# An adaptive-normalisation attention and feed-forward layer: shift weights on ScalarE's queue, first products in turn, weight parts and batch 1's order changed

## The chip, the cores and the metric

One core of a Trainium2 chip. The metric is the device time of one execution, in microseconds (us). The time before is 363.78 us, the median of three runs (363.32 to 365.0).

## What is computed

Four batches of 512 tokens with 512 features, all in float32. `c` (4 x 512) gives six rows per batch: shift and scale of the attention part, its gate, and the same for the feed-forward part.

```python
mod = (_silu(c) @ wmod).reshape(4, 6, 1, -1)
sa, ca, ga, sb, cb, gb = (mod[:, i] for i in range(6))
ga, gb = ...                               # sign kept, magnitude at least 0.25
h = _layernorm(x) * (1 + ca) + sa
x = x + ga * attn(h)
h = _layernorm(x) * (1 + cb) + sb
x = x + gb * ffn(h)
# attn: Xn = layernorm(h)*gamma+beta; Q, K, V = Xn @ W_in + b_in; K, V turned by rotary
#   A = sum over tokens of cos_sim(K) * cos_sim(V); A = 0.5*A + 0.5
#   (A * Q) @ W_out + b_out + h
# ffn: relu(x @ W_up.T) @ W_down.T + (sum of the two top routing weights) * (x @ W_expert)
```

## The kernel before

TensorE multiplies in a float32 form of reduced precision, so each product is three: every operand is split into a high part (a rounded copy, written by ScalarE or GpSimd) and a low part (the rest, written by VectorE or GpSimd), and hi x hi, hi x lo and lo x hi are added. Weights are split in four parts of 128 rows (k = 0 to 3), tokens stand in four tiles of 128 (t = 0 to 3).

Every engine has its own hand-written order, and semaphores alone tie them. SyncE (SP) issues all transfers in the order of its program. The stages are: a start, attention of batches 0 to 3, feed-forward of batches 0 to 3. On TensorE attention(b) is: K/V tile 0 of batch b, the four output rows of batch b-1, K/V tiles 1 to 3, four Q chunks with the eight transposes of batch b+1 between them, and the sums that give A. Tile 3 uses the pair of banks of tile 1, and waits for VectorE's last product step of tile 1 (`krot`, L873); the transposes of chunks 2 and 3 (L1284) wait for the same step of tile 3.

The start. For batch 0 the scale and shift rows are computed on every partition by TensorE from the column `sc0` (silu of c): `mod_first` (L1233 to L1237) does four products for the scale row (bank 2) and then four for the shift row (bank 3), each as two matmuls in full float32. Each product waits for its own 256 KB part of the weights (`ca_w`, `sa_w`). ScalarE adds one to the scale row (L711), VectorE takes the statistics of token rows (`x0_stats`, L1051 to L1056), forms (x - mean) * scale (`scale_row0`, L1061) and then h = that * rstd + shift (`h_row0`, L1074); VectorE's order is statistics of rows 0, scale_row0(0), statistics of rows 1, h_row0(0). Then come second statistics, GpSimd's reciprocal root (L411), z on ScalarE (L626), TensorE's transposes (L1270), gamma and beta (L585), the high copy (L588) and the low split (L842) that the first K/V product needs.

The weights of K and V come in eight parts. High copies are ScalarE's (`split_hi_kv`, L577), low parts GpSimd's (`low_kv`, L414), except part 2 of K, which is VectorE's (`split_lo_kv`, L1079).

Batch b+1's x is normalised in two steps during attention(b). The first: statistics, root on GpSimd (`rstd_x`), shift factors on VectorE (`x_shift`), z on ScalarE (`normalise_x`, L617); GpSimd multiplies by ca (`scale_rows`, L470), VectorE adds sa (`h_row`, L815), and the second normalisation follows. Batch 3's first step is done early, within attention(1): ScalarE sums rows and squares with accumulating passes (`x_sums`, `x_squares`, L596 and L604), VectorE forms mean and variance (L793, L797), and ScalarE writes its z at the end of its attention(1), ahead of batch 1's q evacuation (L648). Meanwhile GpSimd also finishes half of the output rows of batch b-1 (`x2_out`, L453 and L455).

## Time and profile before

| | |
|---|---|
| median of the timed runs | 363.78 us |
| the profiled execution's own time | 365.14 us |
| its span | 363.4 us |
| TensorE busy | 353.1 us |
| VectorE, ScalarE, GpSimd busy | 247.9, 159.1, 126.6 us |
| granted TensorE clock | full speed throughout |

The span runs from the first to the last recorded instruction; a little of the execution lies around it. TensorE is the engine to watch: where it doesn't wait, nothing that other engines do moves the end. In the timeline each line has a start and a duration in us, and in brackets how long the engine idled ahead of it and what released it; "issue" there is a release that the profile doesn't name. A shared port or a lock shows as the same instruction with a longer duration.

### The profile page before, as it was taken

What the parts mean: (1) busy time and instruction counts of PE and PEld (TensorE: products, weight loads), DVE (VectorE), ACT (ScalarE), POOL (GpSimd) and SP (SyncE); (2) the same over time, 40 slices, a digit from 0 to 9 for tenths busy, and PEclk for the clock granted to TensorE, in tenths of its full rate; (3) what the DMA queues carried; (4) which work ended last, traced back from release to release, by engine and by line L of the source; (5) the groups of instructions that cost most, each with busy time, mean ns of one, the idle gap of its engine ahead of it and who ended that gap; (6) DMA issues with size and microseconds to landing.
All of it is one profiled execution on the core that took longest, in us unless ns stands there. A gap on an engine that the chain in (4) does not pass through costs nothing.

```text
span 363.4 us, 4952 instructions
## 1 busy us (share of the span) xinstructions
PE 353.1 (97%) x1794; PEld 288.5 (79%) x1794; DVE 247.9 (68%) x508; ACT 159.1 (44%) x301; POOL 126.6 (35%) x131
## 2 busy tenths in 40 slices
PE   8799999999999999999999999999999999999996
PEld 5257587788777788888888898988988898889885
DVE  2689999979977778786977469338623852382474
ACT  1296838647169501476018753444234423441110
POOL 0395879777726166243531324800100010000000
PEclk9999999999999999999999999999999999999999
DMA  6998482370120000000000003101100110011003
GB/s 182 388 406 317 194 318 89 137 213 0 25 63 2 0 2 29 1 1 2 0 31 0 0 2 115 32 0 58 60 0 2 58 59 2 0 60 58 2 1 115
DMA packets 10985, 27.45 MB, mean 76 GB/s; under 512 B 1216, under 2 KB 1600, under 8 KB 9808
## 3 DMA queue, kind: packets, MB, share of 16 engines
q1 hardware_dynamic: 10960, 27.13, 21.1%
q8 instruction: 14, 0.23, 0.3%
q14 instruction: 11, 0.09, 0.1%
HBM read 22.90 MB, written 4.23 MB: 75 GB/s over the span
## 4 chain that ended last, share of the span: by engine, by line
PE 60%; DVE 12%; ACT 8%; issue 7%; DMA 5%; POOL 5%; SPq 2%; POOLq 0%; DVEq 0%; ACTq 0%
PE ps L1225 19%; PE ps L1227 19%; PE ps L1226 19%; PE ps L1284 2%; DMA gate_bc<-mod_rows 2%; DMA xs<-in_X 2%; POOL w_lo L414 2%; DVE hb L815 1%; DVE hst L825 1%; ACT z L626 1%; POOL hrs L411 1%; ACT ps L638 1%; DMA mod_rows<-xs 1%; ACT ps L585 1%; ACT z L617 1%
## 5 line engine op out<-in xcount | busy, mean ns | idle before, releaser
L1225 PE MATMUL ps<-wv_hi,t_hi 128*128 128x260 f32 (+1 forms) x192 | 61.7, 322 | 0.9 <-POOL wv_lo L414 0.5
L1227 PE MATMUL ps<-wv_hi,t_lo 128*128 128x260 f32 (+1 forms) x192 | 61.4, 320 | 0.0
L1226 PE MATMUL ps<-wv_lo,t_hi 128*128 128x260 f32 (+1 forms) x192 | 61.4, 320 | 0.0
L1225 PE MATMUL ps<-w_hi,g_hi 128*128 128x512 f32 (+1 forms) x132 | 51.2, 388 | 0.0
L1225 PE MATMUL ps<-t_hi,w_hi 128*128 128x512 f32 x128 | 50.6, 396 | 0.1
L1227 PE MATMUL ps<-w_hi,g_lo 128*128 128x512 f32 (+1 forms) x132 | 50.6, 383 | 0.0
L1226 PE MATMUL ps<-w_lo,g_hi 128*128 128x512 f32 (+1 forms) x132 | 50.6, 383 | 0.0
L1227 PE MATMUL ps<-t_hi,w_lo 128*128 128x512 f32 x128 | 50.0, 390 | 0.0
L1226 PE MATMUL ps<-t_lo,w_hi 128*128 128x512 f32 x128 | 49.9, 390 | 0.0
L1225 PEld LDWEIGHTS ps<-wv_hi,t_hi 128*128 128x128 f32 x192 | 36.1, 188 | 5.1 <-POOL wv_lo L414 1.4
L411 POOL TENSOR_TENSOR hrs<-hve,expo 128x4 f32<-128x4 f32 (+2 forms) x12 | 11.1, 923 | 81.9 <-DVE hve L832 62.8
L1227 PEld LDWEIGHTS ps<-wv_hi,t_lo 128*128 128x128 f32 x192 | 36.1, 188 | 2.9
L1226 PEld LDWEIGHTS ps<-wv_lo,t_hi 128*128 128x128 f32 x192 | 36.1, 188 | 2.8
L1225 PEld LDWEIGHTS ps<-w_hi,g_hi 128*128 128x128 f32 x132 | 24.8, 188 | 5.1 <-DVE g_lo L907 0.5
L1227 PEld LDWEIGHTS ps<-w_hi,g_lo 128*128 128x128 f32 x132 | 24.8, 188 | 4.9
L1226 PEld LDWEIGHTS ps<-w_lo,g_hi 128*128 128x128 f32 x132 | 24.8, 188 | 4.7
L1227 PEld LDWEIGHTS ps<-t_hi,w_lo 128*128 128x128 f32 x128 | 24.0, 188 | 5.1
L1225 PEld LDWEIGHTS ps<-t_hi,w_hi 128*128 128x128 f32 x128 | 24.1, 188 | 5.0 <-issue 0.4
L1142 DVE SCALAR_TENSOR_TENSOR g_lo<-ps,g_hi 128x512 fp32r<-128x512 f32 x16 | 11.1, 692 | 24.7 <-ACT g_hi L655 24.6
L1226 PEld LDWEIGHTS ps<-t_lo,w_hi 128*128 128x128 f32 x128 | 24.1, 188 | 4.7
L571 ACT ACTIVATE sqj<-ps 128x512 bf16<-128x512 f32 x16 | 9.5, 591 | 41.5 <-DVE ps L854 36.5
L1225 PE MATMUL ps<-w_hi,t_hi 128*128 128x512 f32 x64 | 26.1, 408 | 1.2 <-DVE prod L873 0.9
(153 smaller groups left out, 703.8 us busy)
## 6 DMA issues: line engine op xcount, KB each, us to landing
stage<-in_w SPq DMA_DIRECT2D x5, 1024.0 KB, 4.8
out<-xs SPq DMA_DIRECT2D x15, 256.0 KB, 2.0
xs<-in_X SPq DMA_DIRECT2D x3, 1024.0 KB, 9.5
xs<-in_wmod SPq DMA_DIRECT2D x8, 256.0 KB, 5.9
stage<-in_w SPq DMA_DIRECT2D x8, 256.0 KB, 8.1
xs<-in_wmod SPq DMA_DIRECT2D x2, 1024.0 KB, 7.7
gate_bc<-mod_rows SPq DMA_DIRECT2D x8, 256.0 KB, 3.9
gate_bc<-in_wmod SPq DMA_DIRECT2D x1, 1024.0 KB, 13.3
```

Of the source, the lines that this page charges most:

```text
L411: nc.gpsimd.tensor_tensor(hrs[:, t0:t0 + n], hve[:, t0:t0 + n], expo[:, 0:n], ALU.pow).then_inc(hrs_s, n)
L414: nc.gpsimd.tensor_tensor(w_lo_of(W_ORDER[i], k), w_raw[i][:, k * D:(k + 1) * D], w_hi_of(W_ORDER[i], k).bitcast(f32), ALU.subtract).then_ ...
L571: nc.scalar.activation(sqj[:], src, ACT.Square, accum_out=nsq[:, t % 2, i:i + 1]).then_inc(nsq_s, 1)
L585: nc.scalar.activation(part, part, ACT.Identity, bias=col[:, COL_BETA + c:COL_BETA + c + 1], scale=col[:, COL_GAMMA + c:COL_GAMMA + c + 1] ...
L617: nc.scalar.activation(z[:, t, :], xs[:, tok(g, t)], ACT.Identity, bias=xnm[:, t:t + 1], scale=xrs[:, t:t + 1]).then_inc(xn_s, 1)
L626: nc.scalar.activation(z[:, t, :], src, ACT.Identity, bias=hnm[:, t:t + 1], scale=hrs[:, t:t + 1]).then_inc(z_s, 1)
L638: nc.scalar.activation(whole, whole, ACT.Identity, bias=bias, scale=scale).then_inc(t_full, 1)
L1142: v.scalar_tensor_tensor(g_lo[:, c, :], ps[:, U_BANKS[c % 2], :], 0.0, g_hi[:, c, :].bitcast(f32), ALU.max, ALU.subtract).then_inc(u_los, 1)
L1225: mm(dst, l_hi, r_hi, start=start, stop=False)
L1226: mm(dst, l_hi, r_lo, start=False, stop=False)
L1227: return mm(dst, l_lo, r_hi, start=False, stop=stop)
L1284: last = nc.tensor.transpose(ps[:, t_bank(g, c), t * P:(t + 1) * P], z[:, t, c * P:(c + 1) * P], idn[:])
```

## The change

SP issues two scale parts, then token rows 0, two scale parts and token rows 1, and no shift parts. ScalarE issues the four shift parts on its own queue ahead of everything else it does. TensorE's first products go scale 0, shift 0, scale 1, shift 1, scale 2, scale 3, then shift 2, shift 3; the scale row is signalled after six products.

GpSimd does K's low part 1 ahead of the root for token rows 2 and 3. V's low part 3 goes from GpSimd to VectorE, between h_row0(3) and the split of transposed rows 1. ScalarE copies V's high part 1 ahead of z of rows 1. One wait in `split_lo_kv` stands twice.

Batch 3's first normalisation moves from attention(1) to attention(2), and is done as batch 2's: statistics on VectorE between q splits, root on GpSimd behind batch 2's bias rows, z on ScalarE behind the first sums. ScalarE's eight accumulating passes and VectorE's mean and variance go. In batches 1 and 2, h row 0 of the next batch goes from behind the sum of tile 0 to behind the product step of tile 1.

```diff
             sp.dma_start(col[:], cols).then_inc(col_in, 16)
...
+            load_scale(0)
+            load_scale(1)
             load_x0(0)
-            for k in range(NC):
-                sp.dma_start(x_slot(3)[:, k * D:(k + 1) * D], wmod[0][:, k * D:(k + 1) * D]).then_inc(sa_w[k], 16)
+            load_scale(2)
+            load_scale(3)
             load_x0(1)
...
                     weight(b, 1)
-                    if b + 2 < B:
-                        rstd_x(b + 2)
                     rstd_h(b + 1, 0, NT)
...
                     for t in range(NT):
                         base(b + 1, t)
+                    if b == 1:
+                        rstd_x(3)
...
             shift_h0(1)
+            low_kv(0, 1)
             rstd_x0(2)
-            low_kv(0, 1)
             low_kv(1, 1)
             low_kv(1, 2)
             low_kv(0, 3)
-            low_kv(1, 3)
             shift_h0(2)
...
                 norm_sums(b, 0)
-                if b == 1:
-                    normalise_x(2)
-                    x_sums()
-                    x_squares()
+                if b < B - 1:
+                    normalise_x(b + 1)
                 norm_sums(b, 1)
...
                     t_evac(b + 1, c)
-                if b + 2 < B:
-                    normalise_x(b + 2)
+            for k in range(NC):
+                nc.scalar.dma_start(x_slot(3)[:, k * D:(k + 1) * D], wmod[0][:, k * D:(k + 1) * D]).then_inc(sa_w[k], 16)
             act.wait_ge(col_in, 16)
...
             split_hi_kv(0, 1)
+            split_hi_kv(1, 1)
             normalise(0, 1, 1)
-            split_hi_kv(1, 1)
...
                 for c in range(NC):
                     q_split(b - 1, c)
-                    if b == 1:
-                        x_row_stats(2, c)
-                if b == 1:
-                    x_aggr(2)
+                    if b < B - 1:
+                        x_row_stats(b + 1, c)
+                if b < B - 1:
+                    x_aggr(b + 1)
                 kv_rows(b, 0)
                 kv_products(b, 0)
-                if b == 1:
-                    x_shift(2)
+                if b < B - 1:
+                    x_shift(b + 1)
...
                 finish_rows(b - 1)
-                if b == 1:
-                    x_mean()
                 kv_sum(b, 0)
-                if b < B - 1:
-                    h_row(b + 1, 0)
-                else:
+                if b == B - 1:
...
                 kv_rows(b, 1)
-                if b == 1:
-                    x_var()
                 kv_products(b, 1)
                 if b < B - 1:
+                    h_row(b + 1, 0)
                     h_row(b + 1, 1)
...
                 kv_products(b, 2)
-                if b + 2 < B:
-                    x_shift(b + 2)
                 kv_sum(b, 2)
...
                 dve.wait_ge(whi_v if i else whi_k, k + 1)
+                dve.wait_ge(wlo_v if i else wlo_k, k)
                 dve.wait_ge(wlo_v if i else wlo_k, k)
...
             h_row0(3)
+            split_lo_kv(1, 3)
             t0_split(1)
...
+            def first_rows():
+                for k in range(2):
+                    first_scale(k)
+                    first_shift(k)
+                for k in range(2, NC):
+                    last = first_scale(k)
+                last.then_inc(bc_ps, 1)
+                for k in range(2, NC):
+                    last = first_shift(k)
                 last.then_inc(bc_ps, 1)
...
-            mod_first(2, x_slot(2), ca_w)
-            mod_first(3, x_slot(3), sa_w)
+            first_rows()
```

## Rows read from the trace of the kernel before

**Rows 1.** busy time (us and share of the span) and instructions of each engine
```profile
PE 353.1 (97%) x1794; PEld 288.5 (79%) x1794; DVE 247.9 (68%) x508; ACT 159.1 (44%) x301; POOL 126.6 (35%) x131
```

**Rows 2.** waits of TensorE's weight loads, 90 to 125 us: total, times, longest
```profile
PEld ps L1225 <- issue: 1.3, 1, 1.3
PEld ps L1284 <- issue: 1.0, 1, 1.0
PEld ps L1284 <- ACT z L626: 0.9, 1, 0.9
PEld ps L1225 <- DVE g_lo L907: 0.5, 1, 0.5
```

**Rows 3.** the same view, 20 to 66 us
```profile
PEld ps L1225 <- POOL wv_lo L414: 1.4, 2, 0.7
```

**Rows 4.** timeline of the first 15 us: start, duration, engine, line, operation
```profile
2.63 0.22 ACT L708 ACTIVATE sc_t<-col 128x16 f32<-128x16 f32 x1 [0.62 <-DMA col<-in_cols]
...
3.54 2.14 SPq L298 DMA_DIRECT2D xs<-in_wmod  x4
...
5.43 3.66 PE L1236 MATMUL ps<-xs,prod 128*128 128x512 f32 x8
...
9.19 0.75 ACT L711 ACTIVATE ps<-ps,half 128x512 f32<-128x512 f32 x1 [6.34 <-PE ps L1236]
...
10.41 3.70 PE L1236 MATMUL ps<-xs,prod 128*128 128x512 f32 x8 [1.33 <-DMA xs<-in_wmod]
...
13.17 0.69 DVE L1051 BATCH_NORM_STATS2 xst<-xs 128x6 f32<-128x512 f32 x1 [2.45 <-DMA xs<-in_X]
...
14.22 0.75 DVE L1074 SCALAR_TENSOR_TENSOR hb<-hb,xrs,ps 128x512 f32<-128x512 f32 x1
```

**Rows 5.** stretches: busy time by engine, clock, DMA share, GB/s
```profile
0.00:7.00 7.00, 5.90 (x14) 4.06 (x15) 1.48 (x10) 1.50 (x2) 0.52 (x5) 1.00 0.63 181
7.00:9.00 2.00, 2.00 (x5) 0.57 (x3) 0.43 (x1) 0.00 (x0) 0.00 (x0) 1.00 0.79 180
9.00:12.00 3.00, 1.67 (x5) 0.86 (x5) 1.35 (x4) 0.75 (x1) 0.56 (x1) 1.00 1.03 386
```

**Rows 6.** timeline, 20 to 29 us
```profile
20.56 0.71 POOL L381 TENSOR_TENSOR xrs<-xve,expo 128x2 f32<-128x2 f32 x1
...
21.36 1.30 POOL L414 TENSOR_TENSOR w_lo<-stage,w_hi 128x512 fp32r<-128x512 f32 x1
...
24.11 0.68 DVE L1079 TENSOR_TENSOR w_lo<-stage,w_hi 128x512 fp32r<-128x512 f32 x1
...
24.30 1.66 POOL L414 TENSOR_TENSOR wv_lo<-stage,wv_hi 128x512 fp32r<-128x512 f32 x1 [0.38 <-ACT wv_hi L577]
...
28.50 0.19 PEld L1225 LDWEIGHTS ps<-wv_hi,t_hi 128*128 128x128 f32 x1 [0.71 <-POOL wv_lo L414]
```

**Rows 7.** timelines of VectorE and GpSimd, 87 to 98 us
```profile
87.60 1.50 POOL L455 TENSOR_TENSOR xs<-xs,hb 128x512 f32<-128x512 f32 x1
87.86 1.79 DVE L815 TENSOR_TENSOR hb<-hb,sa_bc 128x512 f32<-128x512 f32 x1
...
93.61 0.42 DVE L873 TENSOR_TENSOR prod<-ps,rot_sb 128x256 f32<-128x256 f32 x1
...
96.37 1.27 DVE L815 TENSOR_TENSOR hb<-hb,sa_bc 128x512 f32<-128x512 f32 x2
```

**Rows 8.** timeline of ScalarE, 104 to 117 us
```profile
104.37 1.51 ACT L626 ACTIVATE z<-hb,hnm,hrs 128x512 f32<-128x512 f32 x2
...
113.93 2.92 ACT L617 ACTIVATE z<-xs,xnm,xrs 128x512 f32<-128x512 f32 x4
```

**Rows 9.** timeline of VectorE, 137 to 158 us
```profile
137.43 0.70 DVE L854 TENSOR_TENSOR ps<-ps,bkv_bc 128x512 f32<-128x512 f32 x1 [2.57 <-PE ps L1227]
...
156.85 0.42 DVE L873 TENSOR_TENSOR prod<-ps,rot_sb 128x256 f32<-128x256 f32 x1
```

**Rows 10.** the chain that ended last: start, duration, piece
```profile
157.61 0.88 PE ps L1284 x8
```

More of the change, by code:

```diff
@@ L102, in build @@
         nmu = xmn
-        xss = sb("xss", [P, NT])
         xst = sb("xst", [P, NT, 6])
@@ L288, in _, with load_scale @@
             sp.dma_start(col[:], cols).then_inc(col_in, 16)
-            for k in range(NC):
+            def load_scale(k):
                 sp.dma_start(x_slot(2)[:, k * D:(k + 1) * D], wmod[1][:, k * D:(k + 1) * D]).then_inc(ca_w[k], 16)
@@ L294, in load_x0 @@
                              x_batch[0][:, rows0, :]).then_inc(x0_in[i], 16)
+            load_scale(0)
+            load_scale(1)
             load_x0(0)
-            for k in range(NC):
-                sp.dma_start(x_slot(3)[:, k * D:(k + 1) * D], wmod[0][:, k * D:(k + 1) * D]).then_inc(sa_w[k], 16)
+            load_scale(2)
+            load_scale(3)
             load_x0(1)
@@ L589, in t0_evac @@
                                      ACT.Copy).then_inc(t_his, 1)
-            def x_sums():
-                act.wait_ge(x_in, (B - 1) * 16)
-                for t in range(NT):
-                    wait(act, xsum_s, t)
-                    nc.scalar.activation(xjunk[:], xs[:, tok(B - 1, t)], ACT.Identity,
-                                         accum_out=xsum[:, t:t + 1]).then_inc(xsum_s, 1)
-            def x_squares():
-                act.wait_ge(xmn_s, 1)
-                for t in range(NT):
-                    act.wait_ge(xsum_s, NT + t)
-                    nc.scalar.activation(xjunk[:], xs[:, tok(B - 1, t)], ACT.Square, bias=xmn[:, t:t + 1],
-                                         accum_out=xss[:, t:t + 1]).then_inc(xsum_s, 1)
             def normalise_x1(t):
@@ L1231, in idle_products, with first_scale, first_shift @@
                     mm(ps[:, IDLE_BANK, 0:2 * P], acc[:, 0:P], acc[:, 0:2 * P], start=True, stop=True)
-            def mod_first(bank, src, sems):
-                for k in range(NC):
-                    pe.wait_ge(sems[k], 16)
-                    last = mm(ps[:, bank, :], sc0[:, k, :], src[:, k * D:(k + 1) * D], start=(k == 0), stop=(k == NC - 1))
+            def first_scale(k):
+                pe.wait_ge(ca_w[k], 16)
+                return mm(ps[:, 2, :], sc0[:, k, :], x_slot(2)[:, k * D:(k + 1) * D], start=(k == 0), stop=(k == NC - 1))
+            def first_shift(k):
+                pe.wait_ge(sa_w[k], 16)
+                return mm(ps[:, 3, :], sc0[:, k, :], x_slot(3)[:, k * D:(k + 1) * D], start=(k == 0), stop=(k == NC - 1))
+            def first_rows():
[7 more added lines that the diff above has]
+                    last = first_shift(k)
                 last.then_inc(bc_ps, 1)
```

15 lines of the change are left out of this document (1 added, 14 removed).

## The prediction

> **What bounds the kernel now.** I read the table of busy time first: TensorE is busy in 97% of the span [rows 1]. So time can only come from three places: before its first real product, from its waits, or after its last one. The tail is untouched by this change. The waits of its weight loads in the stretch of batch 1 are few: 1.3 us, 1.0, 0.9 and 0.5, 3.7 us in all [rows 2]. In the start, the loads wait 1.4 us more for the low parts of V's weights [rows 3]. Then I read the timeline of the first 15 us: the first token rows become h at 14.22, and everything up to the first K/V product hangs on that as one serial chain over VectorE, GpSimd, ScalarE and TensorE (statistics, root, z, transposes, evacuation, split). So the change has some 6 us to work on, in three places, and in each I ask what is late next.
>
> **Part 1, the first rows (start of h at 14.22).** Before, four scale products are over when ScalarE adds one at 9.19; the four shift products start at 10.41, take 3.70 us (0.9 each) and end at 14.1. VectorE gets its second token rows only at 13.17, takes three short steps (0.69 and two more, about 1.05 to 14.22) and starts h [rows 4]. Two things are thus late together: the shift row at 14.1, and the statistics of token rows 1, which stand ahead of h in VectorE's order.
>
> The change removes the four shift issues from SP's queue (2.14 us for four, 0.54 each [rows 4]) so what is behind them is issued up to 2.1 us sooner, and puts them on ScalarE ahead of its exponential. That began at 2.63 after 0.62 us of idling [rows 4], so it moves by up to 2.14 - 0.62 = 1.5 us; TensorE's first product was at 5.4 and becomes some 0.2 to 0.4 later, 5.7. What it adds on the path is order: TensorE now does scale, shift, scale, shift, scale, scale before the scale row is ready. That is six products instead of four, so at best 5.7 + 6 x 0.9 = 11.1 instead of 9.1. Behind it stand ScalarE's 0.75, VectorE's product of the same kind as that at 14.22 (0.75), and then the 1.05 of statistics that used to be done while VectorE waited for data: 11.1 + 0.1 + 0.75 + 0.75 + 1.05 = 13.8. The best case is -0.4.
>
> Whether TensorE can run at that pace is a matter of bytes. Bandwidth was 181 GB/s over the first 7 us, 180 in the next two and 386 after [rows 5]: 1.27 MB by 7.0, 1.63 by 9.0, 2.79 by 12.0. The transfers up to token rows 1 are 2.65 MB, so their bytes were in by 11.6 and the wait for them ended at 13.17: 1.5 us between byte and wait. Shared evenly by two queues, the last scale part comes after all shift parts and token rows 0, at 2.36 MB instead of 1.05. By the old curve that is 10.9 + 1.5 = 12.4, last scale product over at 13.3, and h at 13.3 + 2.7 = 16.0: +1.8. If the slow stretch of 7 to 9 us vanishes because both queues are in flight early, it lands near 10.8 to 11.2. The trace has no second queue, so both ends stay. I take a landing of 10.8, a last scale product ending at 11.8, h at 14.5: **+0.3** (range -0.4 to +1.8). The Trainium skill (DMA: Bandwidth & Descriptors, "Issuing engines are not separate DMA queues") says that transfers of all issuing engines run on the same 16 engines and interleave, so that a second issuer saves only the time of issuing. No second issuer is in this trace to agree or not; by that rule the late end, with nothing but issue time gained, is the more natural, and it is a rival below.
>
> **Part 2, the order of weight parts.** GpSimd did the reciprocal root for token rows 2 and 3 at 20.56 (0.71 us), in time it had anyway, since K's part 1 could start only at 21.36. Now it waits for that part, works 1.30 on it and does the root at 22.6 to 23.3. VectorE's h of token rows 2 becomes 1.1 us later, and with it VectorE's part 2 of K (24.11). That then meets GpSimd's V part 2, which already took 1.66 instead of 1.30 beside it [rows 6]; I let it wait to 25.9 and end at 26.5, 1.7 late. K's part 3 on GpSimd waits for it and ends at 26.5 + 1.3 = 27.8. Against that, V's part 3 (1.30 on GpSimd, 0.68 on VectorE) leaves GpSimd, where it let TensorE wait 0.71 before the product at 28.50 [rows 6], and lies on VectorE behind h of token rows 3 (27.95) and ahead of the split of t: ready at 28.65, the split at 29.3. The second tile starts at 29.4 where it started three products after 28.50, at 29.1: **+0.3**. Without the collision each step is 0.6 earlier and it is -0.3. Taking V's part 1 before the second normalisation costs nothing: TensorE transposes those rows only after part 0's six products. The repeated wait is one that is already met.
>
> **Part 3, batch 1.** Eight ScalarE passes over batch 3, the mean and the variance go from here; their successor is four statistics on VectorE between batch 1's q splits. What TensorE waited 1.3 us for [rows 2] is VectorE's product step ending at 93.61 + 0.42 = 94.03 [rows 7]. Ahead of that step VectorE loses the mean (0.9), the variance and one h row of 1.79 (the row of 87.86), so it ends near 91.3, 2.7 sooner, and this wait of 1.3 is gone whole. But what is next? That h row is not gone, it comes right behind the step, where GpSimd has four or five products in a row. A VectorE instruction whose two inputs are both in SBUF took 1.79 beside GpSimd's at 87.60, and 1.27 for two, 0.64 each, with none beside it [rows 7]. Going through both engines' orders by turns: h row 0 ends at 92.6, h row 1 at 94.4, GpSimd's last scaling moves by 1.0 to 95.7, h rows 2 and 3 end at 96.9 instead of 97.64. So of 2.7 us only some 0.8 survive. z of batch 2, ending at 105.88 [rows 8], released the transposes (the 0.9 wait); it moves by 0.8, and TensorE, now 1.3 ahead, waits again. The 1.0 wait, for tile 3's product step, gives 0.1 more since the shift for batch 3 went from there. Part 3 is **-0.9** (range -0.65 to -2.05; the far end is no collision at all). The Trainium skill (SBUF — State Buffer, "Who interferes with whom") has it that a VectorE instruction with two SBUF inputs and a GpSimd instruction that reads SBUF shut each other out whole. The trace agrees (1.79 against 0.64), and it speaks against this move of the h row.
>
> **Part 4, batch 3's normalisation out of ScalarE's way.** Its 2.92 us stood at 113.93, right ahead of batch 1's q work [rows 8]. Gone from there, q can begin once its scale is ready, about 0.7 sooner; the splits keep ScalarE's pace with the statistics between, as the trace of batch 0 has them. TensorE's wait of 0.5 for the last split goes: **-0.4** (range 0 to -0.4). The normalisation is now in batch 2 behind the first sums, where ScalarE idles; the new 0.45 of aggregation lies on VectorE before tile 0 of batch 2, which TensorE doesn't wait for.
>
> **Part 5, the price in batch 2.** The same h row was in VectorE's idle time there: it idled 2.57 before the K rows of 137.43 [rows 9]. Now it comes behind the product step and moves all that follows by 0.64. GpSimd's chain gets 0.3 easier or harder. Tile 3's product step ended at 156.85 + 0.42 = 157.27 and TensorE's transposes went at 157.61 [rows 9, 10]: cover 0.2 to 0.3. It comes 0.3 to 0.9 late: **+0.5** (range +0.1 to +0.9). TensorE's other work in batches 2 and 3 and the feed-forward part hangs on nothing that changed.
>
> **Sum.** +0.3 + 0.3 - 0.9 - 0.4 + 0.5 = -0.2. The profiled execution took 365.14 us, of which 363.4 is its span; the median of the timed runs is 363.78, 1.4 below it. The change acts within the span: 363.4 - 0.2 = 363.2, and 363.78 - 0.2 = **363.6** for the median.
>
> **Rivals.** (a) The engines don't collide as I let them. Part 3 is then -2.05 (limited by z of batch 2), part 2 -0.3, part 5 +0.1, part 1 0, part 4 -0.4: -2.65, 361.1. For it: only some of VectorE's instructions show the long form. Against: every h row beside GpSimd does. (b) The scale row comes late. Its place is TensorE's order: the last two scale products now stand behind two shift products, and share bandwidth with all four shift parts. Its price is +1.8 in part 1, sum +1.3, 365.1; it makes part 1 a loss from the point where the sixth product ends after 11.5, and the whole a loss from about 11.9. This is the skill's rule of one set of engines taken at its word. (c) The second queue doesn't do what it is for: its shift parts land no sooner than before, when the first let TensorE begin at 10.41 and the second was used 0.9 later [rows 4]. Then shift 1, scale 2 and scale 3 follow from 11.3, the scale row is done at 14.0, h starts 2.7 later at 16.7, +2.5, sum +2.0, 365.8.
>
> **Chances.** My sum 0.52, (a) 0.28, (b) 0.13, (c) 0.07. The range takes in (a) and (b) and stops at (c): 361.0 to 365.6. A measurement here can tell about 0.5% (1.8 us) from no change. Faster by more needs most of (a): 0.28. Slower by more needs (c), or (b) with the bad end of part 2 or 5: 0.13. Within: 0.59.
>
> **What would show it.** Part 1: the ends of the sixth and eighth first products (11.8, 13.7) and the start of h (14.5). Part 2: K's part 2 on VectorE late by over 1 us, the second tile near 29.4 plus the shift of part 1. Part 3: no wait at 94, but one of about 0.9 before the transposes near 105. Part 4: no wait in the first output rows of batch 1. Part 5: a new wait of about 0.5 before the transposes near 157. I am wrong at once if VectorE's h rows in batch 1 run at 0.64 beside GpSimd, or if TensorE's first six products end by 11.1.

## The result, and the profile after

The changed kernel takes 367.56 us (median of 5 runs, 366.93 to 367.82) where the kernel before took 363.78 (362.38 to 365.0): 1.009 times as long, with an interval of 1.0072 to 1.0108. It is 3.8 us slower by the medians and 3.3 by the ratio, which is taken over more runs of the kernel before, and lies above the predicted range. Its profiled execution took 367.82 us with a span of 365.9.

Its busy times, in the form of [rows 1]:

```profile
PE 355.1 (97%) x1794; PEld 289.7 (79%) x1794; DVE 249.8 (68%) x516; ACT 153.1 (42%) x285; POOL 124.4 (34%) x130
```

TensorE is recorded busy 2.0 us longer for the same 1794 instructions, and again 97% of the span: what is lost must be looked for in its waits and its pace, not in work that was added. The timeline of the first 17 us of after, as in [rows 4]:

```profile
0.73 1.85 ACTq L687 DMA_DIRECT2D xs<-in_wmod  x4
...
4.15 0.22 ACT L689 ACTIVATE sc_t<-col 128x16 f32<-128x16 f32 x1 [0.25 <-DMA col<-in_cols]
...
5.79 1.75 PE L1198 MATMUL ps<-xs,prod 128*128 128x512 f32 x2
...
7.38 1.02 PE L1202 MATMUL ps<-xs,prod 128*128 128x512 f32 x2
...
9.02 0.30 PEld L1198 LDWEIGHTS ps<-xs,prod 128*128 128x128 f32 x2 [1.45 <-DMA xs<-in_wmod]
...
11.38 0.30 PEld L1198 LDWEIGHTS ps<-xs,prod 128*128 128x128 f32 x2 [1.20 <-DMA xs<-in_wmod]
...
12.04 0.49 PEld L1198 LDWEIGHTS ps<-xs,prod 128*128 128x128 f32 x2 [0.37 <-DMA xs<-in_wmod]
...
13.20 1.88 PE L1202 MATMUL ps<-xs,prod 128*128 128x512 f32 x4
...
14.25 0.75 DVE L1022 SCALAR_TENSOR_TENSOR hb<-xs,xmv,ps 128x512 f32<-128x512 f32 x1 [2.61 <-ACT ps L692]
...
14.91 0.69 DVE L1012 BATCH_NORM_STATS2 xst<-xs 128x6 f32<-128x512 f32 x1
...
15.97 0.75 DVE L1035 SCALAR_TENSOR_TENSOR hb<-hb,xrs,ps 128x512 f32<-128x512 f32 x1
```

The reader sees the second queue being issued first (ACTq, 0.73 to 2.58), the exponential moved from 2.63 to 4.15, the products in pairs, and waits of the weight loads for scale parts: 1.45 us before 9.02 (part 1), 1.20 before 11.38 (part 2) and 0.37 before 12.04 (part 3). VectorE's scaling of the token rows starts at 14.25 where it was 9.97, the statistics of token rows 1 come behind it, and h starts at 15.97 instead of 14.22.

The weight parts in after, as in [rows 6] (GpSimd's root, VectorE's h of token rows 2, K's part 2, and K's part 3):

```profile
24.34 0.70 POOL L381 TENSOR_TENSOR xrs<-xve,expo 128x2 f32<-128x2 f32 x1
...
25.07 0.75 DVE L1035 SCALAR_TENSOR_TENSOR hb<-hb,xrs,ps 128x512 f32<-128x512 f32 x1 [1.19 <-POOL xrs L381]
...
26.93 1.19 DVE L1041 TENSOR_TENSOR w_lo<-stage,w_hi 128x512 fp32r<-128x512 f32 x1
...
28.26 1.30 POOL L414 TENSOR_TENSOR w_lo<-stage,w_hi 128x512 fp32r<-128x512 f32 x1 [0.69 <-DVE w_lo L1041]
```

The root and the h row that waits 1.19 for it, the 1.19 of K's part 2 beside GpSimd, and GpSimd's wait of 0.69 for it are as the prediction let them run. The waits of the weight loads from 90 to 125 us, as in [rows 2]:

```profile
PEld ps L1260 <- issue: 1.0, 1, 1.0
PEld ps L1260 <- ACT z L609: 0.7, 1, 0.7
```

The 1.3 and the 0.5 are gone, and 1.7 us stay. In batch 1 and at the end of batch 2 (VectorE's K rows, product step and h rows of batch 1; TensorE's transposes of batch 2):

```profile
91.28 0.70 DVE L822 TENSOR_TENSOR ps<-ps,bkv_bc 128x512 f32<-128x512 f32 x1 [2.67 <-PE ps L1190]
...
95.20 0.42 DVE L841 TENSOR_TENSOR prod<-ps,rot_sb 128x256 f32<-128x256 f32 x1
...
95.55 1.92 DVE L783 TENSOR_TENSOR hb<-hb,sa_bc 128x512 f32<-128x512 f32 x2
...
159.75 0.86 PEld L1260 LDWEIGHTS ps<-idn,z 128*128 128x128 f32 x8 [0.69 <-issue]
```

Two h rows beside GpSimd took 1.92 us, where two alone take 1.27 [rows 7]: the collision is there. So is the new wait near the end of batch 2, 0.69 us. And VectorE now idles 2.67 us before the K rows at 91.28, since TensorE has not made them yet.

Where the 3.8 us are: the start of single steps in the timelines (us from the span's start; the last row is an end). "h" is VectorE's first h row; all rows of transposes are TensorE's weight loads for them. "Transposes 1a, 1b" are the two groups in which TensorE transposes z of batch 1 in the middle and at the end of batch 0's attention, and so on. before (2) is a second profiled execution of the kernel before (363.72 us in all), taken with the experiments.

| step | before | before (2) | after | after less before (2) |
|---|---|---|---|---|
| h of token rows 0 | 14.22 | 14.32 | 15.97 | +1.65 |
| first K/V product | 21.55 | 21.64 | 24.53 | +2.89 |
| transposes of z, third 128 tokens | 30.48 | 30.53 | 32.28 | +1.75 |
| transposes 1a | 56.36 | 56.42 | 58.57 | +2.15 |
| transposes 1b | 60.66 | 60.72 | 64.12 | +3.40 |
| transposes 2a | 105.93 | 104.48 | 108.14 | +3.66 |
| transposes 3a | 153.61 | 152.18 | 155.48 | +3.30 |
| transposes 3b | 157.39 | 155.93 | 159.75 | +3.82 |
| end of the last product | 360.25 | 358.84 | 362.59 | +3.75 |

Three things are read from it. The loss lies in the start (+1.65) and between transposes 1a and 1b (+1.25), and +0.5 in between. The changes of batch 1 and later gave nothing (+3.40 to +3.75). And the first K/V product is 2.9 us late for a moment, of which 1.75 are left at the third tile. The stretches of after, in the form of [rows 5], and the weight loads around them:

```profile
15.00:20.00 5.00, 3.04 (x16) 0.90 (x16) 4.69 (x11) 1.82 (x3) 2.52 (x4) 1.00 1.05 388
20.00:22.00 2.00, 2.00 (x9) 0.55 (x8) 1.93 (x8) 1.68 (x6) 1.78 (x2) 0.69 1.05 402
22.00:25.00 3.00, 3.00 (x10) 2.43 (x11) 1.57 (x4) 3.00 (x6) 2.08 (x3) 0.64 1.00 410
```

```profile
19.71 0.42 PEld L1246 LDWEIGHTS ps<-idn,z 128*128 128x128 f32 x4 [2.84 <-issue]
...
21.71 2.79 PEld L1194 LDWEIGHTS ps<-acc 128*128 128x128 f32 x8 [1.28 <-issue]
...
24.53 0.19 PEld L1188 LDWEIGHTS ps<-w_hi,t_hi 128*128 128x128 f32 x1
```

Behind a gap of 2.84 us of the weight loads, ahead of 19.71, the granted clock falls to 0.69 and 0.64, a mean of time at the 1.2 GHz level (0.50) and time at 2.4 GHz, where before had 1.00 (2.4 GHz) throughout. The idle products of the load at 21.71 (products whose results nobody uses) take 2.79 us at it. What that costs is an experiment below.

### The profile page after: what moved, and what is told of

The parts are those of the page before. It is cut to its first block, busy times and chain, and to the rows that moved or that the text cites. A ratio compares the mean times of both kernels' runs of the same rounds, so it can differ in the third digit from the quotient of the medians.

```text
span 365.9 us, 4943 instructions
## 1 busy us (share of the span) xinstructions
PE 355.1 (97%) x1794; PEld 289.7 (79%) x1794; DVE 249.8 (68%) x516; ACT 153.1 (42%) x285; POOL 124.4 (34%) x130
## 4 chain that ended last, share of the span: by engine, by line
PE 59%; DVE 19%; issue 10%; ACT 5%; DMA 2%; POOL 2%; SPq 0%; POOLq 0%; DVEq 0%; ACTq 0%
PE ps L1188 19%; PE ps L1190 18%; PE ps L1189 18%; PE ps L1260 2%; DMA xs<-in_wmod 2%; DVE hb L783 2%; ACT z L609 2%; DVE prod L835 2%; DVE ps L839 1%; POOL hrs L411 1%; DVE hst L793 1%; DVE hst L787 1%; ACT sqj L570 1%; DVE acc L853 1%; ACT z L600 1%
```

## The experiments

The kernels of a group ran on one chip with runs of the kernel before beside them; its median was 363.6 to 364.5 us from group to group, so each kernel is compared with the one of its group.

**The three parts, one at a time.** start_only has the second queue, SyncE's new order and the new order of products; parts_only the new order of weight parts; batch_only all of batch 1 and later.

> Before, with only the first part: shift weights from ScalarE's queue and the eight first products in turn. Theory A (the late scale row is most of the loss): h of the first token rows starts near 16.0 instead of 14.2, TensorE is at half clock for its idle products, and the time is 2.0 to 2.6 us above before. Theory B (the weight parts are most of it, by loading VectorE in the start): the late start is mostly absorbed by the waits on weight parts, at most +1.0. Theory C (a collision of VectorE and GpSimd near 60 us adds 1.1 us, and comes only with all parts together): +1.5 to +1.9.

> Before, with only the second part: order of the weight parts. Theory A: +0.3 to +0.9, since the root of token rows 2 and 3 comes 2 us later and VectorE's part 2 of K collides with GpSimd. Theory B: +1.5 or more. Theory C: 0 to +0.3.

> Before, with only the third part: batch 3's first normalisation in attention(2) and h row 0 behind tile 1's product step in batches 1 and 2. All theories: the wait of 1.3 us near 94 goes, the one of 0.5 near 122 goes, a new one of 0.4 to 0.7 comes near 157: 0.9 to 1.3 us below before. If the start and this part depend on each other (the gate rows' round trip), it is between 0 and 0.6 below.

| kernel | median | before | ratio (interval) | difference |
|---|---|---|---|---|
| start_only | 366.29 | 364.51 | 1.0053 (1.0033 to 1.0072) | +1.9 |
| parts_only | 365.80 | 364.51 | 1.0045 (1.0029 to 1.0061) | +1.6 |
| batch_only | 364.59 | 364.51 | 1.0001 (0.9981 to 1.0020) | 0.0 |

The differences by the ratios add up to 3.5, where the whole change has 3.3 by its ratio. That they fit so well is partly chance: start_only and parts_only both contain the loss between transposes 1a and 1b, which after has only once (below). The start costs more than its likely value, the weight parts five times theirs, and batch 1 gains nothing of what all theories expected. Each needs its cause.

**The same kernels once more, for a second trace.** before_again is the kernel before, batch_again is batch_only, both unchanged.

> Before unchanged, for a second trace of it. Theory C (near 58 us VectorE's sum of tile 2 and GpSimd's low part 1 of the output weights ask for the shared port within 0.05 us of each other, so executions of before differ): this trace may show the sum at 1.0 or at 2.1 us, and the wait of 1.3 us near 94 may be missing; its end then lies 0.6 to 1.4 us before that of the first trace. If before is steady, both traces agree within 0.3 us at every stage.

> The third part alone, unchanged, for a second trace. Its profiled time lay 0.7 us under its median. If the third part really is worth 1.2 us, this trace repeats the first within 0.3 us; if it gains only against a slow execution of before, this one differs from its first trace by 0.5 us or more, in the stage before 65 us.

before_again took 363.72 us in its profiled execution, batch_again 365.14. The waits of the weight loads in before_again, 90 to 125 us:

```profile
PEld ps L1285 <- issue: 0.9, 1, 0.9
PEld ps L1285 <- ACT z L627: 0.5, 1, 0.5
PEld ps L1226 <- DVE g_lo L908: 0.5, 1, 0.5
```

The wait of 1.3 us on which part 3 rested [rows 2] isn't there. The profiled execution of before was a long one of its kind (365.14 us against a median of 363.78), and this is where it lost its time: in it VectorE had waited 1.46 us for the gate rows, which come back from memory, as this row of its timeline shows:

```profile
79.51 1.29 DVE L916 TENSOR_TENSOR hb<-ps,hb 128x512 f32<-128x512 f32 x2 [1.46 <-DMA gate_bc<-mod_rows]
```

In before_again that wait is absent, and transposes 2a start 43.76 us after 1b instead of 45.27. In all other traces of this study that distance is 43.3 to 44.0, but for late_old, below. (The sum at 57.7 us, where the expectation looked for the difference, is short in both traces of before.) Between batch_only and batch_again the difference is elsewhere, at the sum of tile 2 of batch 0 (VectorE L885 of before) against GpSimd's second low part of the out weight. before_again:

```profile
57.73 1.02 DVE L886 SCALAR_TENSOR_TENSOR acc<-prod,wgt,acc 128x768 f32<-128x768 f32 x1
57.77 2.12 POOL L407 TENSOR_TENSOR w_lo<-stage,w_hi 128x512 fp32r<-128x512 f32 x1
```

batch_again:

```profile
57.34 2.15 DVE L849 SCALAR_TENSOR_TENSOR acc<-prod,wgt,acc 128x768 f32<-128x768 f32 x1
57.39 1.29 POOL L403 TENSOR_TENSOR w_lo<-stage,w_hi 128x512 fp32r<-128x512 f32 x1
```

Both engines start within 0.05 us of each other. In the one VectorE takes 1.02 us and GpSimd's instruction is the long one (2.12 for 1.29), in the other VectorE takes 2.15. Transposes 1b follow 4.30 us after 1a in before_again and 5.56 in batch_again, and the end comes 1.2 us later than in batch_only (360.25 against 359.02). The same kernel does both, so this is decided from execution to execution. The starts don't tell which way it goes: VectorE is 0.04 to 0.05 us ahead in every trace of either form.

**Which engine goes first.** after has the long form:

```profile
59.88 2.14 DVE L853 SCALAR_TENSOR_TENSOR acc<-prod,wgt,acc 128x768 f32<-128x768 f32 x1
59.92 1.28 POOL L406 TENSOR_TENSOR w_lo<-stage,w_hi 128x512 fp32r<-128x512 f32 x1
```

after_win is after with a wait that lets VectorE's sum go first; before_win is the same in before.

```
                 pool.wait_ge(whi_out, k + 1)
+                if k == 1:
+                    pool.wait_ge(kacc, 3)
```

> The changed kernel, with GpSimd made to wait for VectorE's sum of tile 2 of batch 0 before its low part 1 of the output weights, so that VectorE has the shared port first. Theory C: the sum takes 1.0 us instead of 2.1, the transposes near 64 come 1.0 us sooner and the time is 0.7 to 1.1 below the changed kernel's, 366.5 to 366.9. Theories A and B: another wait takes its place, within 0.3 of the changed kernel's 367.6.

> The kernel before, with GpSimd's second low part of the out weight held until VectorE's sum of tile 2 is done. Theory C (which engine gets the shared port at 57.7 us is decided within 0.05 us and is worth 1.2 us): in the executions of before that VectorE wins nothing changes; in those it loses 1.2 us are saved. The sum takes 1.02 us in the profile, the end is that of before or up to 0.6 us sooner, and the spread of the runs is narrower; total 0 to 0.8 us below before. Rival: before always wins the port, and the wait only delays GpSimd: total equal or 0.3 us over before.

after_win took 366.49 us (1.0058, 1.0044 to 1.0073), 1.1 less than after, and its sum runs short:

```profile
60.02 1.02 DVE L855 SCALAR_TENSOR_TENSOR acc<-prod,wgt,acc 128x768 f32<-128x768 f32 x1
...
61.18 1.30 POOL L408 TENSOR_TENSOR w_lo<-stage,w_hi 128x512 fp32r<-128x512 f32 x1 [1.20 <-DVE acc L855]
```

before_win took 363.77 against 363.58 (1.0007, 0.9989 to 1.0024): no difference, within 0.9 us. So before seems to have the short form mostly by itself. The long form is in the traces of start_only, parts_only, queue_only, queue_late, sp_order, order_only, after and after_warm (transposes 1b 5.55 to 5.57 us after 1a), the short one in before, before_again, batch_only and late_old (4.29 to 4.30). All traces whose h begins at 14.8 or later and that lack the added wait have the long form; of the earlier ones, parts_only (14.21) and batch_again (13.93) have it too. That a late start tips the order is thus likely; how it does so isn't shown.

With this the traces can be added up, against before_again. after's 3.75 us are 1.65 at h, 0.50 from there to transposes 1a, 1.25 from the long form and 0.35 behind transposes 1b. start_only has 1.25, 0.06, 1.26 and 0.09 at these places, parts_only -0.11, 0.50, 1.26 and 0.09, batch_only -0.42, 0.03, -0.01 and 0.58. The weight parts by themselves are thus about 0.5, and their timed +1.6 is for the most part the order at 58 us; and the changes of batch 1 and later cost some 0.35 to 0.6 behind transposes 1b, which the timed 0.0 is too coarse to show (its interval is 0.7 to either side).

**The first rows: what makes the scale row late.** queue_only has the queue and SyncE's new order but the old order of products. order_only has the new order of products and everything on SyncE. queue_late is queue_only with ScalarE's four issues behind its exponential. sp_order has SyncE's new order alone (token rows 0 ahead of scale parts 2 and 3), late_old the late second queue alone:

```
 sp_order                          late_old
 load_scale(0); load_scale(1)      # SyncE: scale 0..3, then
 load_x0(0)                        load_x0(0)
 load_scale(2); load_scale(3)      load_x0(1)
 # shift parts 0..3, load_x0(1)    # ScalarE, behind exp: shift 0..3
```

> Shift weights on ScalarE's queue and SP's new order, but products as before: four scale, then four shift. Theory A1 (the shared bandwidth makes the last scale part late): its landing is at 12 or later, the scale row is ready near 12.9, h starts at 15.4 to 15.8, time +1.2 to +2.0. Theory A2 (the order of the products makes it late): the last scale part lands by 10.5 and h starts at 14.2 or before, time 0 to -0.5.

> All eight first products' weights stay on SyncE, scale parts ahead of shift parts as before; only TensorE's order changes (two scale and two shift products in turn, then scale 2 and 3, then shift 2 and 3). Theory A1 (the start was lost because the scale parts share the transfer time with shift parts on a second queue): with one queue the scale parts land as before (about 4.5 us), but the first shift product now stands ahead of the third scale product and its part is issued fifth, at about 6 us, so the last scale product ends about 0.4 us later and h row 0 begins at 14.2 to 14.7; total within 0.5 us of before. Rival A2 (the loss lies in the alternation, which delays the scale row whatever the queues do): h row 0 begins at 15.5 or later, as in the run of part 1 alone (15.57), and the total is 1.5 us or more over before.

> As the run queue_only (shift parts on ScalarE's own queue, products in the old order), but ScalarE issues them behind its exponential, at about 3.0 to 4.9 us instead of 0.7 to 2.6. Theory A1 (the early shift parts take transfer time from the scale parts, and the exponential and with it the first product are pushed back): the exponential is at 2.6 again, the first product at 5.4 to 5.6, all four scale products run with waits of under 0.5 us in all, h row 0 begins at 13.5 to 14.7 instead of 16.88, total within 1 us of before. Rival A3 (a second queue costs whatever its moment): h row 0 begins at 16 or later and the total is 2 to 4 us over before.

> Only SyncE's own order is changed: token rows 0 are issued ahead of the third and fourth scale part; the shift parts stay on SyncE behind them. Theory F1 (the late landing of scale parts 2 and 3 comes from the token rows that now stand ahead of them): in the trace the third and fourth scale product wait as in queue_late (1.5 us and 0.5), the scale row is done near 12, h row 0 begins at 15.0 or later, total 0.8 to 1.5 us over before. Theory F2 (it comes from the second queue's bytes): with one queue the scale products wait 0 to 0.6 us more than before, the shift row is still what sets h row 0, which begins at 14.2 to 14.8, total within 0.5 us of before.

> ScalarE issues the four shift parts on its queue behind its exponential, and SyncE keeps its old order otherwise: all four scale parts first, then token rows. Theory F1: scale parts land as before, the scale row is done by 9.2 to 9.6, h row 0 begins at 13.2 to 14.3, total 0 to 0.9 us below before. Theory F2: the shift parts of the second queue still take transfer time from the last scale parts, which land near 8.5 and 10, and h row 0 begins at 14.7 to 15.5, total 0.5 to 1.5 us over before.

From the timelines: the start of ScalarE's addition (the scale row is done) and of h of token rows 0, and the timed difference by the ratio. Six more traces have the start of before, so that there are eight: the scale row at 8.84 to 10.16, h at 13.58 to 14.32. That is how far one kernel varies.

| kernel | second queue | SyncE's order | products | scale row | h | time |
|---|---|---|---|---|---|---|
| before | no | old | old | 9.19 | 14.22 | |
| before_again | no | old | old | 10.10 | 14.32 | |
| late_old | late | scale first | old | 10.58 | 14.01 | +0.9 |
| sp_order | no | new | old | 11.26 | 14.80 | -0.2 |
| queue_late | late | new | old | 12.03 | 15.46 | +1.8 |
| start_only | early | new | new | 13.07 | 15.57 | +1.9 |
| queue_only | early | new | old | 13.45 | 16.88 | +4.0 |
| after | early | new | new | 13.47 | 15.97 | +3.3 |
| order_only | no | old | new | 17.61 | 20.11 | +5.9 |

Each edit delays the scale row against the two traces of before: SyncE's order by 1.2 to 2.1 us, the late second queue by 0.5 to 1.4, both by 1.9 to 2.8, and with ScalarE issuing early by 3.3 to 4.3. All lie above the eight traces; which of the first two is the larger is not settled by one trace each. The waits of queue_only's weight loads, and its scale row:

```profile
8.48 0.30 PEld L1242 LDWEIGHTS ps<-xs,prod 128*128 128x128 f32 x2 [2.45 <-DMA xs<-in_wmod]
...
11.36 0.30 PEld L1242 LDWEIGHTS ps<-xs,prod 128*128 128x128 f32 x2 [2.58 <-DMA xs<-in_wmod]
...
13.45 0.75 ACT L717 ACTIVATE ps<-ps,half 128x512 f32<-128x512 f32 x1 [9.22 <-PE ps L1242]
```

The second scale product stands behind 2.45 us of waiting and the third behind 2.58: already part 1, the second transfer that SyncE issued for the rows, is late. In sp_order and late_old, the longest wait of the same loads, the scale row, and h:

```profile
10.03 0.30 PEld L1240 LDWEIGHTS ps<-xs,prod 128*128 128x128 f32 x2 [2.35 <-DMA xs<-in_wmod]
...
11.26 0.75 ACT L715 ACTIVATE ps<-ps,half 128x512 f32<-128x512 f32 x1 [8.64 <-PE ps L1240]
...
14.80 0.75 DVE L1078 SCALAR_TENSOR_TENSOR hb<-hb,xrs,ps 128x512 f32<-128x512 f32 x1
```

```profile
9.35 0.30 PEld L1236 LDWEIGHTS ps<-xs,prod 128*128 128x128 f32 x2 [1.92 <-DMA xs<-in_wmod]
...
10.58 0.75 ACT L711 ACTIVATE ps<-ps,half 128x512 f32<-128x512 f32 x1 [7.74 <-PE ps L1236]
...
14.01 0.75 DVE L1074 SCALAR_TENSOR_TENSOR hb<-hb,xrs,ps 128x512 f32<-128x512 f32 x1
```

Their scale rows are 1.2 to 2.1 and 0.5 to 1.4 us later than before's, and yet h moves by 0.6 at most. Between them stand the shift products, which had a wait to lose, and token rows 1. In late_old, queue_late and queue_only h begins 3.43 us after the scale row, with the start of before 3.7 to 5.1: there h has other things to wait for, and 0.3 to 1.7 us of lateness of the scale row are hidden. With both edits this slack is used up. sp_order fits F2 (h 14.2 to 14.8, time within 0.5), late_old's time fits F2 as well, but its h fits F1. So F1 and F2 are both half right: the two delays roughly add, and neither alone moves h beyond 0.6. A1 was right that the landing of scale parts is what makes the row late, and wrong that the moment of issue is the whole of it (queue_late was expected at 13.5 to 14.7 and came at 15.46); A3 wanted 16 or later and is wrong too. For queue_only, A1 expected the scale row near 12.9, h at 15.4 to 15.8 and +1.2 to +2.0, and fell short (13.45, 16.88, +4.0); A2 had the wrong sign. The times of sp_order, queue_late, queue_only, start_only and order_only may also hold the long form at 58 us, which their traces have; sp_order's trace is of its longest execution (365.54 us, median 363.76).

The order of products has its own story. In order_only the first shift product waits for a part that SyncE issues behind the four scale parts and token rows 0:

```profile
10.01 2.08 PE L1239 MATMUL ps<-xs,prod 128*128 128x512 f32 x2 [3.37 <-DMA xs<-in_wmod]
```

```profile
5.00:10.00 5.00, 1.64 (x4) 0.50 (x3) 1.03 (x3) 0.00 (x0) 0.56 (x1) 0.91 0.98 316
10.00:15.00 5.00, 4.99 (x6) 2.19 (x7) 0.00 (x0) 0.00 (x0) 0.00 (x0) 0.50 1.05 393
```

TensorE stood still from about 6.6 us to 10.01, and the granted clock is 0.50 from 10 to 15 us, the 1.2 GHz level. The next products start at 11.88, 13.59 and 15.29, so three of them take 1.76 us each instead of 0.92 [rows 4], 2.5 us in all; the 3.37 us of standing still are the rest of the 5.8 to 5.9 by which h is later. A1 expected h at 14.2 to 14.7 and is wrong here. A2 (15.5 or later) has the sign, but not the rule that alternation costs whatever the queues do: beside the early second queue it gives back 0.8 to 1.4 us of h (15.47 to 16.11 in the four traces with it, queue_only 16.88), since two shift products then fill waits for scale parts: h begins 2.50 us after the scale row instead of 3.43.

**The slow clock at 20 to 25 us.** after_warm is after with four more idle products behind those of the other modulation rows (`mod_pair`) and ahead of the transposes of z of tile 0, so that TensorE doesn't stand still before 19.7.

```
             mod_pair((0, 1, 2))
+            idle_products(4)
```

> The kernel after with four more idle products behind the three rows of products of z of tile 0, so that TensorE does not stand idle for 2.8 us at 17 to 20 us. Theory D (the half clock at 20 to 25 us, granted 0.64 to 0.69, is what puts the first K/V product at 24.53): granted clock 1.00 there, first K/V product at about 23.3, but the second tile only 0 to 0.3 us earlier, since the weight parts set its time; total 0 to 0.4 us below the kernel after (367.56), so still 3.4 us or more over before. Rival (the clock's loss is carried to the end): total 1.0 to 1.3 us below the kernel after. Third possibility: the extra products are in the way and change nothing or cost up to 0.5 us.

The granted clock was 1.00 throughout, and the first K/V product came at 22.79 instead of 24.53. But the transposes of the third tile started at 31.77 against 32.28 and the last product ended at 362.10 against 362.59, which is what h itself was sooner in this execution (15.47 against 15.97), and the time was 367.54 us (1.0101, 1.0081 to 1.0120) against 367.56. This is theory D. The clock's fall is real and costs nothing that is seen at the end: in after the K/V products behind it wait for weight parts (0.47, 0.21 and 0.16 us between 28.1 and 30.3).

**Batch 1: where the gain went.** batch_h_win is batch_only with batch 3's h row 0 at its old place in batch 2 and with the wait of after_win. h_both has the h row at its old place in batch 1 too, where VectorE idles 2.67 us in after:

```
 kv_sum(b, 0)
-if b == B - 1:
+if b < B - 1:
+    h_row(b + 1, 0)
+else:
     ...
 kv_products(b, 1)
 if b < B - 1:
-    h_row(b + 1, 0)
     h_row(b + 1, 1)
```

> The change's batch 1 part alone (start and weight parts as before), with batch 3's h row 0 left at its old place behind the sum of tile 0 of batch 2, and with GpSimd's wait of the run after_win. If the gains and costs of part 3 to 5 are as the traces read (batch 3's z out of the way -0.4, the h row's new wait near 157 +0.5, the port's tie 1.2 in some executions): the wait near 157 shrinks from 0.7 to under 0.3 us, the time from the third to the fourth pair of transposes of batch 2 to 3 is 3.8 again instead of 4.3 to 4.5, and the total is 0.4 to 1.4 us below before. Rival (the h row's wait is the same work moved, and comes back elsewhere): total within 0.3 us of before.

> The change's batch 1 part alone, with h row 0 of the next batch left at its old place (behind the sum of tile 0) in batch 1 as well as in batch 2, and with GpSimd's wait of the run after_win. Theory E (part 3 gave nothing because VectorE, rid of the mean and the variance, now idles 2.7 us before the K rows of tile 1 and has the h row to do behind the product step, where its chain to the root and z of the next batch is the one that TensorE waits for): the idle 2.7 before the K rows shrinks to about 0.9, the last statistics of batch 2 end 0.6 to 1.3 us sooner, the transposes near 104 come 0.3 to 0.8 us sooner relative to those near 60, total 0.4 to 1.2 us below before. Rival (something else binds TensorE there, such as GpSimd's own chain of scaled rows): the distance from the transposes near 60 to those near 104 stays 44.0, total within 0.3 us of before.

batch_h_win took 364.11 us against 363.58 (1.0007, 0.9991 to 1.0022): the rival, no difference. The wait near the end of batch 2 stayed at 0.63, and the distance from transposes 3a to 3b went from batch_only's 4.47 to 4.20, not to before_again's 3.75. So the h row is 0.27 of that price at most: in after, which has it moved, the distance is 4.27, only 0.07 more than in batch_h_win. h_both took 363.56 against 364.47 (0.9978, 0.9964 to 0.9992): 0.9 us less than the kernel before (0.8 by the ratio, 0.3 to 1.3 by the interval). It carries the wait of after_win too, which by itself gave before nothing (before_win). VectorE in batch_h_win (K rows of batch 1, two h rows, last step of the statistics):

```profile
87.34 0.70 DVE L819 TENSOR_TENSOR ps<-ps,bkv_bc 128x512 f32<-128x512 f32 x1 [2.65 <-PE ps L1188]
...
91.63 1.92 DVE L780 TENSOR_TENSOR hb<-hb,sa_bc 128x512 f32<-128x512 f32 x2
...
97.51 0.17 DVE L797 TENSOR_SCALAR hve<-hmv 128x4 f32<-128x4 f32 x1
```

and in h_both (the h row at its old place, the same three):

```profile
85.52 1.77 DVE L780 TENSOR_TENSOR hb<-hb,sa_bc 128x512 f32<-128x512 f32 x1
...
87.61 0.70 DVE L819 TENSOR_TENSOR ps<-ps,bkv_bc 128x512 f32<-128x512 f32 x1 [0.32 <-PE ps L1186]
...
91.61 1.32 DVE L780 TENSOR_TENSOR hb<-hb,sa_bc 128x512 f32<-128x512 f32 x1
...
96.90 0.17 DVE L797 TENSOR_SCALAR hve<-hmv 128x4 f32<-128x4 f32 x1
```

With the h row in the idle time, one h row of 1.32 us is left behind the product step instead of two of 1.92, and the statistics end at 96.90 instead of 97.51, from a start that was 0.3 later. Transposes 2a follow 1b after 43.30 us, against 44.03 in batch_h_win, 43.99 in batch_only and 43.76 in before_again. From 1b to the last product h_both takes 0.57 us less than before_again, though VectorE waited 0.55 us for the gate rows in it. This is theory E: in the changed kernel the mean and the variance leave VectorE, but what they leave is idle time, and the h row that used to lie there is moved onto the chain to z of batch 2.

**The second queue in the faster kernel.**

> The kernel h_both with the four shift parts issued by ScalarE behind its exponential, as in queue_late. If the two edits are independent, the total differs from h_both by what queue_late differs from before: 0 to 0.7 us less by theory A1, 2 to 4 us more by rival A3. The distances between the later transposes are those of h_both within 0.1 us.

> The kernel h_both with the edit of late_old in its start. The total differs from that of h_both as late_old's differs from that of before: by theory F1 0 to 0.9 us less (so 0.9 to 1.8 us below before), by F2 0.5 to 1.5 us more.

h_both_late took 364.53 us (1.0008, 0.9994 to 1.0021) and h_both_old 364.04 against 364.37 (0.9993, 0.9972 to 1.0015). Both lie over h_both's ratio, by 1.1 and 0.5 us, with h at 15.26 and 14.39 instead of 13.87; in the kernel before the same edits cost 1.8 and 0.9. The sign carries over, but the sizes aren't the same thing: queue_late's trace has the long form at 58 us, which h_both_late, with the added wait, can't have, and its own 1.1 is in size the 1.4 us by which its h is later. For h_both_old the intervals overlap with h_both's, so its 0.5 is no more than a tendency. A1, A3 and F1 are wrong here, and F2 is right at its edge. No form of the second queue that was tried gained anything. h_both, with the start of before, is the fastest of all.

## Why the prediction was wrong, step by step

**Part 1, +0.3 predicted, +1.9 timed.** The step that failed is the choice between the two ends of the landing. I took 10.8 for the last scale part's landing and 11.8 for the end of the sixth product. Its product pair began at 11.38 and ended at 13.36, the eighth ended at 15.08 (13.7 was expected), and h began at 15.97: rival (b)'s own numbers, 13.3 and 16.0. The last scale part was waited for until 12.04, near the late end's 12.4. The byte curve was sound and bandwidth did improve as I hoped between 7 and 9 us, where [rows 5] has 180 GB/s (the same stretch of after: 279), but that didn't bring the scale parts: part 1 was waited for until 9.02 and part 2 until 11.38. The extra bytes were probably those of shift parts; the trace doesn't say whose they were. That row of after's stretches:

```profile
7.00:9.00 2.00, 1.40 (x3) 0.30 (x2) 0.00 (x0) 0.00 (x0) 0.00 (x0) 1.00 0.93 279
```

This is what the rule of the Trainium skill that the prediction set against the change says (DMA: Bandwidth & Descriptors, "Issuing engines are not separate DMA queues"), and the runs agree: the scale row's addition by ScalarE went from 8.84 to 10.16 in the eight traces with the start of before to 10.58 and 10.96 by a late second queue alone (late_old, h_both_old). I gave that 0.13, though nothing in the trace spoke for the hopeful end. That (b)'s price of +1.8 is so near the timed +1.9 of start_only is partly luck: in its trace h is 1.25 later, and another 1.26 come from the long form at 58 us, which (b) didn't have. SyncE's own new order stood only inside the byte count of the late end (token rows 0 ahead of the last scale parts) and had no price of its own; alone it delays the scale row by 1.2 to 2.1 us (sp_order), though not the time (-0.2).

**Part 2, +0.3 predicted, +1.6 timed.** Its steps came true one by one: the root behind K's part 1, 1.2 us of waiting for h of token rows 2, K's part 2 in collision (1.16 in parts_only), K's part 3 behind it. The second and third tile hardly moved in parts_only (z of the third tile 30.50 against 30.48). Up to transposes 1a the part cost 0.39, so the price of +0.3 was right for what it covered. The step that failed is that I priced the lateness of VectorE only where TensorE meets it first, and had no term for any later place. At 58 us, where VectorE and GpSimd start within 0.05 us of each other, VectorE's sum took the long form: transposes 1b were 1.65 late in parts_only, 1.26 of it from there. That the order there is worth 1.1 us is shown by after_win. What tips it stays open: VectorE is ahead by the same 0.04 to 0.05 us in both forms, and batch_again had the long one with an early start.

**Part 3, -0.9 predicted, none seen.** Two steps failed. The wait of 1.3 us to be removed was not the kernel's but that execution's: before_again doesn't have it. The prediction saw that the profiled execution was 1.4 us over the median, and subtracted the change from both alike without asking which wait those 1.4 were. And the h row: I said that it comes behind the step, and let only 0.8 of 2.7 us survive. The last step of the statistics moved by -0.17 (97.60 in batch_only for 97.77) from a first h row 0.42 sooner, so nothing survived: the 2.7 us that left VectorE became 2.67 us of idling ahead of the K rows. The collision itself was right (1.92 for two rows beside GpSimd), and so rival (a), which had none, is out.

**Part 4, -0.4 predicted.** Right at its place: the wait of 0.5 in the first output rows is gone, and transposes 3a follow 2b 0.37 sooner (42.96 for 43.33). **Part 5, +0.5 predicted:** transposes 3b follow 3a 0.52 later in after (4.27 for 3.75, with a new wait of 0.69, as the prediction said near 157) and 0.72 later in batch_only. But the two aren't independent, as I had them. With the h row back, 0.45 stayed: VectorE's product step of tile 3 ended only 0.17 sooner (155.22 in batch_h_win, 155.39 in before_again) while TensorE was 0.6 sooner. So TensorE's gain of part 4 seems to have turned into a wait for VectorE's chain at the next place; the h row, which the prediction had as the whole price, adds 0.07 to 0.27.

**The sum.** Timed by parts, +1.9, +1.6 and 0.0 stand against +0.3, +0.3 and -0.8. Rival (b), alone with the wrong side, was right in place for part 1 and near in price, and its sum of 365.1 was short by the order at 58 us (1.1, after_win) and by the gains of batch 1 that it kept (0.8), which gives 367.0. Rival (c) is out: the first shift product began at 7.38 instead of 10.41.

**Left open.** late_old timed 0.9 us over before though its h began 0.3 sooner than before_again's. Its profiled execution has the long way of the gate rows (45.17 us from transposes 1b to 2a, and a wait of 1.35 us for the gate rows), as in the first trace of before. h_both_old, with the same start, waited 0.94 us for them, h_both and h_both_late 0.55 and 0.53, and the other traces show no such wait. Whether it is frequent in late_old, and what decides it, wasn't settled. Open too are what tips the order at 58 us and how often each kernel has which form, since only profiled executions show it.

## What to carry to other kernels

Before pricing a wait as removable, see whether it explains that the profiled execution was longer than the median; if so, take a second trace first. A second issuing queue made no room here: other bytes came in between those that were needed first. So ask of the earliest consumer's last transfer which bytes of all queues may come before it, the old queue's own reordering included. Follow an engine that becomes late until its lateness is absorbed, not only to the first place where the bound engine meets it, and look for places where two engines start almost together: their order may turn. And before moving work, see whether it lies in idle time; moved onto a chain it costs there, and leaves only idling behind.

## What was unexpected of the hardware

- Where VectorE and GpSimd started within 0.05 us of each other, either one could have the long instruction, from execution to execution of one kernel: VectorE's sum took 1.02 us or 2.15, and the end moved by 1.2 us (batch_only and batch_again).
- TensorE's granted clock fell to the 1.2 GHz level after it had stood still: 0.64 to 0.69 as a mean in stretches of after (2.84 us without a weight load before them), 0.50 from 10 to 15 us in order_only (4.20 us without one, 3.37 without a product). With products in the gap it stayed at 1.00 (after_warm). But it isn't the gap alone: order_only has another one of 2.84 us, before 23.85, and the clock was 1.00 from 20 to 30 us. In the first case the fall cost nothing at the end, in order_only 2.5 us.
- Four DMA issues took ScalarE 1.85 us, 0.46 each, ahead of its first work, and 2.23 to 2.82 us behind its exponential. SyncE's issue of scale parts 2 and 3, begun at 2.58 in each, took 0.91 us in sp_order, queue_late and h_both_late, and 1.19 to 2.27 in the five traces in which ScalarE had issued before it (2.04 in after). Why isn't shown.
